# Half of the second feed-forward product in one lump, and the key and value passes in one half head, in a one-core transformer kernel

## The reference, cut

```python
x = x + attn(layernorm(x))        # q, k, v projections, rope, causal
# diff = softmax(q1 k1) - lambda * softmax(q2 k2);  attn = diff @ v
# attn = attn * rsqrt(mean(attn**2) + eps) * w * (1 - lambda_init);  attn @ Wo.T
x = x + ffn(layernorm(x))
# h = gelu(x @ quant(w1).T + b1)     (2048 wide);  out = h @ quant(w2).T + b2
```

## Time and profile before

| | us |
|---|---|
| median of 3 runs | 4307.65 |
| lowest and highest | 4298.69, 4309.7 |
| the profiled execution's own time | 4298.3 |
| its span, first to last instruction | 4296.5 |
| TensorE busy | 3484.7 (81%) |
| VectorE busy | 3382.8 (79%) |
| ScalarE busy | 2880.2 (67%) |
| GpSimd busy | 1437.2 (33%) |

### The profile page before, as it was taken

The page is one execution under the profiler, slowest core; times in us unless marked ns, Lnnn a source line. Parts: engine busy times, 40 slices in busy tenths (PEclk is TensorE's granted clock), DMA queues, the critical chain, the costliest instruction groups (busy, mean ns, idle before and its releaser), DMA issues.

```text
span 4296.5 us, 81536 instructions
## 1 busy us (share of the span) xinstructions
PE 3484.7 (81%) x23454; PEld 2095.0 (49%) x23454; DVE 3382.8 (79%) x6194; ACT 2880.2 (67%) x6784; POOL 1437.2 (33%) x1564
## 2 busy tenths in 40 slices
PE   2688888888888887888788888888878878888886
PEld 1355544455445454545544544445544555444553
DVE  6788977888678886888767887778877889778881
ACT  1577766777567775677756777667766777567772
POOL 1243233332332324433343323432234432333323
PEclk6899999999999999999999999999999999999998
DMA  3100011000011001100011000101011000111000
GB/s 130 41 18 30 19 33 33 31 17 29 25 33 33 18 30 33 33 20 28 21 33 33 26 27 18 39 25 33 20 34 33 25 23 20 34 33 33 15 29 12
DMA packets 146817, 128.38 MB, mean 30 GB/s; under 512 B 66608, under 2 KB 117680, under 8 KB 145840
## 3 DMA queue, kind: packets, MB, share of 16 engines
q1 hardware_dynamic: 146352, 122.79, 8.8%
HBM read 67.61 MB, written 55.12 MB: 29 GB/s over the span
## 4 chain that ended last, share of the span: by engine, by line
PE 41%; DVE 20%; issue 20%; ACT 12%; POOL 5%; DMA 1%; SPq 1%; DVEq 1%; ACTq 1%; POOLq 0%
PE M L837 9%; DVE NM L682 6%; PE M L887 6%; PE SP_ L852 6%; PE F L924 6%; PE F L909 5%; PE DP L864 4%; DVE NM L690 3%; ACT E L554 3%; ACT DT L566 2%; ACT L571 2%; PE M L831 2%; DVE CC L702 1%; PE DX L864 1%; PE SP_ L853 1%
## 5 line engine op out<-in xcount | busy, mean ns | idle before, releaser
L554 ACT ACTIVATE E<-SP_,NM 128x256 f32<-128x256 f32 (+7 forms) x2048 | 1520.4, 743 | 1020.3 <-DVE NM L690 533.8
L852 PE MATMUL SP_<-KST,QST 96*128 96x512 f16 (+3 forms) x3072 | 838.2, 344 | 459.2 <-ACT E L554 385.4
L682 DVE TENSOR_REDUCE NM<-SP_ 128x1 f32<-128x896 f32 (+3 forms) x1024 | 1031.9, 1017 | 225.0 <-PE SP_ L853 218.5
L705 DVE SCALAR_TENSOR_TENSOR E<-E,CC 128x512 f32<-128x512 f32 (+7 forms) x1024 | 942.2, 920 | 36.2
L864 PE MATMUL DP<-ident,E 128*128 128x128 f32 x3328 | 585.1, 292 | 112.8 <-DVE E L705 97.2
L852 PEld LDWEIGHTS SP_<-KST,QST 96*128 96x128 f16 x3072 | 277.9, 101 | 793.8 <-ACT E L554 531.1
L690 DVE TENSOR_REDUCE NM<-SP_ 128x2 f32<-128x1024 f32 (+3 forms) x512 | 419.4, 819 | 244.8 <-PE SP_ L853 239.5
L566 ACT ACTIVATE DT<-DP 128x512 f32<-128x512 f32 (+3 forms) x1024 | 524.8, 513 | 127.8 <-PE DP L864 121.4
L837 PE MATMUL M<-WQKV,WT 128*128 128x512 f32 x1040 | 538.4, 611 | 10.3 <-DVE TOK L746 5.3
L909 PE MATMUL F<-X2H,W1Q 128*128 128x256 f16 x2048 | 501.4, 283 | 39.4 <-ACT HP L613 21.7
L864 PEld LDWEIGHTS DP<-ident,E 128*128 128x128 f32 x3328 | 389.8, 149 | 277.8 <-issue 125.8
(11 more groups left out here) (94 smaller groups left out, 4726.9 us busy)
## 6 DMA issues: line engine op xcount, KB each, us to landing
scratch<-SPL SPq DMA_DIRECT2D x65, 576.0 KB, 2.8
QST<-scratch SPq DMA_DIRECT2D x390, 64.0 KB, 2.4
X<-in_x SPq DMA_DIRECT2D x66, 256.0 KB, 2.7
out<-SQ SPq DMA_DIRECT2D x64, 256.0 KB, 2.0
KST<-scratch SPq DMA_DIRECT2D x390, 32.0 KB, 1.9
DT<-in_w2T SPq DMA_DIRECT2D x1, 4096.0 KB, 25.7
KST<-in_w1T SPq DMA_DIRECT2D x2, 1024.0 KB, 12.0
WQKV<-in_wqT SPq DMA_DIRECT2D x1, 1024.0 KB, 7.1
```

What stands on the lines that cost most here:

```text
L554: act.activation(dst, score_out(i, 2 * n + k, w), ACT.Exp, bias=NM[:, (2 * u + k) % 8:(2 * u + k) % 8 + 1], scale=1.0, accum_out=SUM[:, i ...
L682: nc.vector.tensor_reduce(NM[:, m:m + 1], score_out(i, 2 * n + k, P * (i + 1)), AX.X, ALU.max, negate=True).then_inc(max_ready, 1)
L705: nc.vector.scalar_tensor_tensor(out=E1[:, u % 4, 0:w], in0=E2[:, u % 2, 0:w], scalar=CC[:, u % 4:u % 4 + 1], in1=E1[:, u % 4, 0:w], op0=A ...
L852: pe.matmul(SP_[:, k[a // 512], 0:n], q, KST[0:ROWS, a // P:(a + n) // P, kk, :], start=True, stop=not last)
```

## The change

The second product's first sum is cut in two. Its f 0 to 7 stand all in half head 1 of the even block, right behind the Gelu of f 8 to 15. Its f 8 to 15 are spread over half heads 6 to 15; in half heads 6 and 11 that gives none (hence the new return on an empty range). So f 8 stands in half head 7, where it stood in 11. The second sum stays in half heads 18 to 30. In odd blocks all four key and value passes stand in half head 15, and pieces 4, 5 and 6 of the first product begin in half heads 16, 20 and 24 instead of 15, 19 and 23. In even blocks the passes stay at 13, 14, 15 and 15.

```diff
-KV_PROJ, KV_ROPE = (13, 14, 15, 15), 16
+KV_PROJ, KV_ROPE = ((13, 14, 15, 15), (15, 15, 15, 15)), 16
...
-W1_AT = (1, 4, 7, 11, 15, 19, 23, 27)
+W1_AT = (1, 4, 7, 11, 16, 20, 24, 27)
...
-W2_AT, W2_N = (4, 18), 13
+W2_LUMP, W2_REST, W2_NEXT = 1, (6, 10), (18, 13)
...
     def second_product(self, hs):
 
-        for j, at in enumerate(W2_AT if self.w2 else ()):
-            if at <= hs < at + W2_N:
-                return j, range(FT * (hs - at) // W2_N, FT * (hs - at + 1) // W2_N)
+        if not self.w2:
+            return None
+        if hs == W2_LUMP:
+            return 0, range(0, GELU_F)
+        for j, f0, (at, n) in ((0, GELU_F, W2_REST), (1, 0, W2_NEXT)):
+            if at <= hs < at + n:
+                return j, range(f0 + (FT - f0) * (hs - at) // n, f0 + (FT - f0) * (hs - at + 1) // n)
         return None
...
             def second_product(q, j, fs):
 
+                if not fs:
+                    return
                 if fs[0] == 0:
                     hold(pe, h_ready, 8 * q + 4)
                     hold(pe, hp_ready, 8 * q + 8)
...
-                        if hs == KV_PROJ[0]:
+                        if hs == KV_PROJ[t % 2][0]:
                             after(pe, q_roped, nb + 1)
-                        if hs in KV_PROJ:
-                            project(WQKV, D, [j for j in range(KD) if KV_PROJ[j] == hs], m_kv)
+                        if hs in KV_PROJ[t % 2]:
+                            project(WQKV, D, [j for j in range(KD) if KV_PROJ[t % 2][j] == hs], m_kv)
```

## The result

The changed kernel takes 4312.59 us (median of 20 runs, 4304.68 to 4321.59), the kernel before beside it 4305.45 us (20 runs, 4298.69 to 4318.54): ratio 1.0017 with the interval 1.0010 to 1.0024. That is within the 0.3% that count as no change, and 77 us above the 4236 forecast. The profiled run of the changed kernel took 4309.39 us.

The account below looks back on a forecast made before the run. TensorE (81%) and VectorE (79%) were busy, neither alone bounding; 16 waits cost 52.9 us. Block gains of 9.9 less 0.9 gave 9.0 us a batch, 72 us over eight: 4236 us, own range 4205 to 4268.

Parts of the forecast that it names:

- twelve f become seven: Block 0, half heads 8 to 16: 2.2 us less TensorE work in a stretch without TensorE gaps, gain 2.1 us.
- Rival (a): Split waits eat more; scores, maximum and exponential pace half heads 8 to 16 of blocks 0 and 2: 28 us gain, 4280, chance 0.17.
- the lump: Eight f in half head 1 of even blocks: 3.5 us at full clock, free everywhere; 7.0 us at half clock.
- charge for an overrun in blocks 4 and 6: Eight f wholly at half clock overrun by 1.9 and 1.5 us there; a quarter charged, 0.9 us a batch.
- the wait of half head 7: f 8 waits there for all eight splits: TensorE idle about 1.5 us in block 0, 2.1 us in block 2.
- Rival (d): Slower: the new wait at half head 7 lowers the granted clock in blocks 0, 2 and 4; 50 us slower, 4358, chance 0.05.
- The chance that I gave to that rule: Free-running activity look: either clock level by chance inside the eight f of half head 1; 1.7 us a batch charged, 4242.
- The 0.88 us is worth most of that: Half head 19: piece 5's first half leaves, ending most of VectorE's score waits, 1.59 us in block 5, 0.52 in block 7.
- pieces 4 to 6 come a half head later: Odd blocks: first-product pieces shift, piece 5's first half leaving half head 19; with the clock, block 5 gains 1.5, block 7 0.6.
- the forecast of 0 for blocks 1 and 3: Blocks 1 and 3: the GpSimd chain from Gelu to the next scores holds its length, so 0 us change.
- The passes under the Gelu: Odd blocks, half head 15: 1.0 us more work inside 2.81 us of idle time, no cost; nothing gained in half heads 12 to 14.
- The rule on GpSimd: Less VectorE waiting would lengthen GpSimd splits awaited at half head 7; 0.6 us more in blocks 0 and 2, sum below 10 us.

Follow-up runs that it names:

- the odd part alone: Kernel before, with only odd blocks' key and value passes in half head 15 and pieces 4 to 6 one half head later: 4328.68 us, 1.0042.
- with f left out: Changed kernel with f 8 to 15 in half heads 9 to 16, but f 9 to 14 of the first sum omitted: 4269.75 us, 0.9923.
- piece 4 back: Changed kernel with f 8 to 15 in half heads 9 to 16, piece 6 at 23, odd passes as before, piece 4 at 15: 4269.69 us, 0.9908.
- even blocks alone: Changed kernel with only the second product's new order; key and value passes and first-product pieces as in the kernel before: 4311.12 us, 1.0009.

## Why the prediction was wrong

The forecast was 9.0 us a batch shorter, the blocks came out 1.0 longer. Of these 10 us, about 4 are the thinned half heads 8 to 16, about 4 the odd blocks, and about 2 the granted clock in blocks 2 and 0.

**The step that failed first: "From half heads 8 to 16, twelve f become seven, 2.2 us, in a stretch with no TensorE gap: gain 2.1"**, with 1.7 for block 2 and 1.2 for block 4. Measured: from half head 10 to 18, where four of the f are gone, 0.0 us in block 0 in every batch and in block 2 in five of seven (0.2 and 0.4 longer in the others), and 0.8 in block 4 from half head 8 on. The fewer f stood, net, in half heads 8, 11, 12 and 16; the one of half head 8 gave 0.1 to 0.4 us in block 0 where the clock was full. The premise was that an engine without a gap in its records bounds the stretch. It doesn't: leaving 2.6 us out of that stretch gave 0.9 us in blocks 0 and 2 and 0.3 in block 4. Rival (a) came near: it had the loop pace these half heads once the f are thinned. Its 28 us of gain was still too much, as it left out the clock and the loss in the odd blocks too.

**Right: the lump is free, and the clock comes back.** Eight f hide under the Gelu in every even block, and no charge for an overrun in blocks 4 and 6 shows. But the term was sized as TensorE's saving. By half head 5 to 7 blocks 0, 2, 4 and 6 are ahead by 1.8, 0.6, 0.8 and 0.6 us, where 3.2, 0.5, 1.0 and 0.8 had been counted. In block 0 the lead is 1.0 to 2.2 us by batch: 2.2 in batch 1, where the low clock ends 1.6 us into the block, 1.0 in batch 7, where it ends at 5.8. Even the largest is short of 3.2; that the exponentials can't follow TensorE further is likely, but not shown.

**Right in place and price: the wait of half head 7.** I put 1.5 us in block 0 and 2.1 in block 2; measured are at most 1.2 in block 0, less in the batches in which the low clock behind the Gelu ends later, and 1.9 to 2.35 in block 2. For block 2 I counted 1.0 us later than before, the wait less the head start. Batch 1, without a low stretch, ends 1.2 later. What I had wrong is the clock: the other batches lose another 1.5 to 2.5 us there. Rival (d) named it, a fall of the granted clock at this place, and gave it 0.05, for two blocks of three. It came in block 2 in six batches of seven and in block 0 in two. But the wait is only one of its causes: in four of the six the clock fell before the wait began, and with the wait gone it still fell in two. I weighed the length of the wait against 2.81 us; the rows show what else to look at, that TensorE was busy for just over half of the 7.3 us before the fall, with the f of half heads 4 to 7 taken away.

The Trainium skill, TensorE: Matmul & The Clock Gate, section "What's actually happening", says that the look at activity is free-running. By that rule, the same wait meets the fall or misses it by chance, and the trace agrees: of the three batches of the changed kernel that come to the wait alike and wait 2.35 us, one meets no fall, one meets it in the wait and one behind it. The chance that I gave to that rule was put at the lump, where it changed nothing. It belonged here.

**The second step: the odd blocks.** "The 0.88 us is worth most of that" held: at half head 20 block 5 gains 1.6 us, block 7 about 0.9. But "pieces 4 to 6 come a half head later" was costed for piece 5 alone, and for piece 4 in half head 17, "which hides it". Piece 4 costs 0.7 us at half head 18 of block 5. Piece 6, which I did not cost, lands beside the output projection: 0.9 to 1.5 us at half head 26 of all four odd blocks, of which up to 0.6 comes back in half head 27. Hence the forecast of 0 for blocks 1 and 3, which looked only at the chain from GpSimd, fell too: the wait for the DMA is 51.9 us, as forecast, and moved with its last scores. The passes under the Gelu were right at nothing; they ran mostly at the low clock, for 6.12 us, without harm.

**The rule on GpSimd**, from the Trainium skill, GPSIMD Engine Reference, section Specifications, whose effect I had left out, did not show where it was feared: the last split of block 2 takes 1.15 us against 1.16 in the earlier trace rows:

```profile
1728.26 1.15 POOL L478 TENSOR_TENSOR HL<-HP,HH 128x512 f16<-128x512 f32 x1
```

Over the whole span the three operations of all splits take 675 us where they took 656, and 17 of these 19 us are in blocks 5 and 7; the odd part alone has them too (676 us). Whether that is the rule at work no run here shows.

**Open.** Between kernels that differ only in even blocks, odd ones move by up to a microsecond (with f left out, block 5 by -1.3 and block 7 by +1.1), and low stretches move with them. What decides whether a given batch meets one I can't tell from these runs: in block 2 every kernel with the lump has them, in one batch of seven (piece 4 back) to all seven (even blocks alone), so part of what sets these kernels apart is which batches were hit. A block's number is trusted here only where one half head carries it, or where the batches without a low stretch agree.

## What to carry to other kernels

Price an edit half head by half head, by what ended the wait there: an engine without a gap can be merely keeping up, so that less work on it gives little and more costs most of it. When a list of places is shifted, look for each entry at what it now stands beside, not only at the one the shift is for. And work that is taken out of a stretch to fill a hole elsewhere leaves the stretch thinly used; that, or a short wait put there, may cost more in granted clock than in waiting: here 1.9 us beside 1.4. Before a block's number is read, the batches with a low stretch have to be set apart from those without.

## What the hardware did that I had not expected

The granted clock fell with no long idle time before it: TensorE had been busy for 3.82 of the 7.30 us before, with no gap over 1.32 us, and it fell in some batches of the same program and not in others, after the same work. And in the other direction, eight f at the start of a block ran into the full level within the lump: in block 0 of batch 3 the first matmul took 0.59 us and the last 0.38, and the value products behind it 1.93 where they had taken 3.26.
